# Second-layer experts of a two-layer transformer kernel: weights stand, tokens move, features on partitions

## What is computed

```python
logits = xf @ gate_w + gate_b
scores = softmax(logits)
top_vals, top_idx = top_k(scores, 2)
cw = (one_hot(top_idx, 16) * top_vals[..., None]).sum(axis=1)
h = einsum('td,edh->teh', xf, w1) + b1
g = einsum('td,edh->teh', xf, w3) + b3
a = silu(h) * g
y = einsum('teh,ehd,te->td', a, w2, cw) + cw @ b2
```

## Time and profile before

| | |
|---|---|
| median of 3 runs | 506.08 us (505.69 to 508.32) |
| the profiled execution | 501.9 us, of it the span of the trace 500.2 us |
| TensorE busy, matmuls | 421.4 us (84% of the span), 2573 instructions |
| TensorE busy, weight loads | 316.4 us (63%) |
| VectorE busy | 362.5 us (72%) |
| ScalarE busy | 280.8 us (56%) |
| GpSimd busy | 253.4 us (51%) |
| mean granted TensorE clock | 0.946 of full speed |

### The profile page before, as it was taken

How to read it: one execution, slowest core, us unless ns; L and a number is a source line. 1 busy time by engine, 2 the same in 40 slices (tenths; PEclk the granted TensorE clock), 3 DMA queues, 4 the chain that set the end, 5 groups by cost and what they waited for, 6 DMA issues and landing times.

```text
span 500.2 us, 11175 instructions
## 1 busy us (share of the span) xinstructions
PE 421.4 (84%) x2573; PEld 316.4 (63%) x2573; DVE 362.5 (72%) x1185; ACT 280.8 (56%) x753; POOL 253.4 (51%) x340
## 2 busy tenths in 40 slices
PE   3979762396999999569999999999897969999994
PEld 3567651296999998236556556656554556777774
DVE  5859884052665666489999999999966536777774
ACT  2447540142555554277888888888655245665551
POOL 4014767031545445425545686785666027666562
PEclk9999955597999999799999999999999999999998
DMA  8912425666677686662142161000001321222217
GB/s 230 283 14 56 72 65 116 134 155 166 169 191 209 182 260 203 157 177 72 33 106 68 48 166 55 11 23 11 13 23 43 98 64 46 76 78 80 62 50 227
DMA packets 62321, 53.67 MB, mean 107 GB/s; under 512 B 9677, under 2 KB 51710, under 8 KB 62131
## 3 DMA queue, kind: packets, MB, share of 16 engines
q1 hardware_dynamic: 55330, 42.97, 33.4%
q0 software_dynamic: 5056, 8.48, 5.1%
q10 hardware_dynamic: 1872, 1.52, 1.3%
HBM read 41.15 MB, written 13.73 MB: 110 GB/s over the span
## 4 chain that ended last, share of the span: by engine, by line
PE 28%; DVE 25%; issue 16%; POOL 9%; SPq 9%; DMA 8%; ACT 4%; DVEq 0%; POOLq 0%; ACTq 0%
POOL results L854 6%; PE bank L1847 4%; PE bank L1800 3%; DVE qk_sums L1422 3%; PE bank L1906 3%; PE bank L1815 3%; DVE sums L1445 3%; POOL sorted_tokens L839 3%; PE bank L1946 2%; DVE big L1415 2%; DVE work L1459 2%; SPq L592 2%; SPq L678 2%; DMA results<-work 2%; DMA big<-in_W 2%
## 5 line engine op out<-in xcount | busy, mean ns | idle before, releaser
L854 POOL DMA_INDIRECT results<-work x94 | 92.3, 982 | 96.1 <-DVE work L1379 67.7
L1847 PE MATMUL bank<-late,work 128*128 128x512 f32 x192 | 92.6, 612 | 2.6 <-ACT work L1014 2.4
L990 ACT ACTIVATE work<-bank,mcol 128x128 f32<-128x128 f32 x94 | 43.0, 457 | 72.7 <-PE bank L1792 72.7
L1359 DVE TENSOR_SCALAR work<-bank,b_columns 128x128 f32<-128x128 f32 x94 | 28.7, 347 | 35.9 <-PE bank L1800 35.8
L1847 PEld LDWEIGHTS bank<-late,work 128*128 128x128 f32 x192 | 33.7, 195 | 32.5 <-issue 29.1
L1800 PE MATMUL bank<-work,big 128*128 128x128 f32 x376 | 53.3, 288 | 0.0
L1815 PE MATMUL bank<-big,work 128*128 x376 | 51.0, 280 | 0.1
L1800 PEld LDWEIGHTS bank<-work,big 128*128 128x128 f32 x376 | 49.1, 204 | 0.1
L1815 PEld LDWEIGHTS bank<-big,work 128*128 128x128 f32 x376 | 47.1, 197 | 0.3 <-issue 0.3
L999 ACT ACTIVATE work<-bank,b_columns 128x128 f32<-128x128 f32 x94 | 29.4, 363 | 29.1 <-PE bank L1800 29.1
L1792 PE MATMUL bank<-ident,work 128*128 128x128 f32 x94 | 27.0, 287 | 18.5 <-DMA work<-sorted_tokens 10.2
(11 more groups left out here) (254 smaller groups left out, 1003.5 us busy)
## 6 DMA issues: line engine op xcount, KB each, us to landing
big<-in_W SPq DMA_DIRECT2D x47, 256.0 KB, 2.7
work<-sorted_tokens SPq DMA_DIRECT2D x94, 65.0 KB, 1.9
big<-in_w SPq DMA_DIRECT2D x48, 88.0 KB
big<-results SPq DMA_DIRECT2D x14, 256.0 KB, 3.7
sorted_tokens<-zeros SPq DMA_DIRECT2D x26, 65.0 KB, 2.6
late<-in_WqkvbT SPq DMA_DIRECT2D x1, 1544.0 KB
results<-work POOLq DMA_INDIRECT x94, 2.9
bias_big<-in_b1e SPq DMA_DIRECT2D x16, 88.0 KB
```

Of the source, the lines that this page charges most:

```text
L854: pool.indirect_dma_start(ys[l], bass.IndirectOffsetOnAxis(xg[b][:, D:D + 1].bitcast(I32), 0), yo[b], None, bounds_check=TOPK * T - 1, oob ...
L990: act.activation(xgT[b % 2], bank[:, ends[b % 2], 0:P], ACT.Identity, bias=scale_shift[0], scale=scale_shift[1]).then_inc(e_xTc, 1)
L1847: last = pe.matmul(bank[:, 2 * k + i, :], h3T[b], Wqkvb[:, k * HD + i * 512:k * HD + (i + 1) * 512], start=True, stop=True)
```

## The change

The hidden features of 176 are cut into a part of 112 and a part of 64. The weights of an expert are laid out in four pieces (w1 part A, w3 part A, w3 part C, w1 part C) and stand in TensorE, the tokens move, 128 columns; features come out on partitions. Three products take the place of one: both C parts share the third stationary block (w3's on partitions 0 to 63, w1's on 64 to 127). The activations need no turning back. Biases b1 and b3 are columns: silu takes its bias in ScalarE's instruction, and VectorE adds the other and multiplies in one instruction per part. The output bias b2 is one more row of w2 (row 112) against a row of ones in the activations, which GpSimd writes once. The weights of a slot are copied by VectorE from the looked-up place into a ring of four fixed places, from which TensorE loads them. The order of TensorE's list is now look-up, turn, hidden, output (lag 3). Bias rows come by four more DMAs at the start; the spread biases are no longer loaded (seven DMAs per expert for six).

The diff, cut to its core:

```diff
@@ build
+        HA, HC = 112, H1 - 112
+        parts13 = [(0, 0, HA), (1, 0, HA), (1, HA, HC), (0, HA, HC)]
+        part_at = [0, HA, 2 * HA, 2 * HA + HC]
+        b13r = sb("b13_rows", [E, 2 * H1])
+        NF = 4
+        w13r = sb("w13_ring", [P, NF, 2 * H1])
+        b13c = sb("b13_columns", [P, 3, E])
@@ sync, at the start
+            for (k, a, m), to in zip(parts13, part_at):
+                sp.dma_start(b13r[:, to:to + m], (b1e, b3e)[k][:, a:a + m]).then_inc(ld_w0, 16)
@@ sync, weights1
-                    for k, (w, bias) in enumerate(((w1, b1e), (w3, b3e))):
-                        sp.dma_start(w13v[:, e, k, :], w[e, :, :].rearrange("e d h -> d e h")).then_inc(ld_w1, 16)
-                        sp.dma_start(bv[:, e, k, :], bias[e, :].rearrange("(a e) h -> a e h", a=1)
-                                     .to_broadcast([P, 1, H1])).then_inc(ld_w1, 16)
-                    sp.dma_start(w2s.rearrange("p (e c d) -> p e c d", e=E, c=2)[:, e, :, :],
-                                 w2[e, :, :].rearrange("e (c p) d -> p e c d", p=K1)).then_inc(ld_w1, 16)
-                    sp.dma_start(b2B[:, :].rearrange("p (e d) -> p e d", e=E)[:, e, :],
-                                 b2e[e, :].rearrange("(a e) d -> a e d", a=1).to_broadcast([P, 1, D])).then_inc(ld_w1, 16)
+                    for (k, a, m), to in zip(parts13, part_at):
+                        sp.dma_start(w13v[:, e, to:to + m],
+                                     (w1, w3)[k][e, :, a:a + m].rearrange("e d h -> d e h")).then_inc(ld_w1, 16)
+                    sp.dma_start(w2v[0:HA, e, 0, :], w2[e, 0:HA, :].rearrange("e p d -> p e d")).then_inc(ld_w1, 16)
+                    sp.dma_start(w2v[HA:HA + 1, e, 0, :], b2e[e, :].rearrange("(a e) d -> a e d", a=1)).then_inc(ld_w1, 16)
+                    sp.dma_start(w2v[0:HC, e, 1, :], w2[e, HA:H1, :].rearrange("e p d -> p e d")).then_inc(ld_w1, 16)
@@ gpsimd, between the gates and the diagonals
+            pool.wait_ge(f_one, 2)
+            for b in range(2):
+                pool.memset(hbT[b][P - 32:P, 0:P], 1.0).then_inc(f_one, 1)
+            pool.wait_ge(f_one, 4)
@@ scalar, tokens
-                    after(act, e_h, l * SLOTS + t - 1)
+                    after(act, e_h, l * SLOTS + (1 + l) * (t - 1))
@@ scalar, second layer
-            run_slots(act, SLOTS, NX, [(2, silu), (0, tokens(1, router1["ss"])), (3, act_turned)])
+            def silu_parts(t, b, q, e):
+                act.wait_ge(e_h, SLOTS + 2 * t + 1)
+                after(act, e_act, 2 * (t - 1))
+                act.activation(hb[b % 2][0:HA, 0:P], bank[0:HA, 1 + b % 2, 0:P], ACT.Silu,
+                               bias=b13c[0:HA, 0, bass.ds(e, 1)]).then_inc(e_silu, 1)
+                act.activation(hb[b % 2][0:HC, P:2 * P], bank[P - HC:P, 1 + b % 2, P:2 * P], ACT.Silu,
+                               bias=b13c[P - HC:P, 2, bass.ds(e, 1)]).then_inc(e_silu, 1)
+
+            run_slots(act, SLOTS, NX, [(0, tokens(1, router1["ss"])), (0, None), (1, silu_parts)],
+                      table(mybir.EngineType.Activation, tbl, P, E - 1))
@@ vector, ahead of the first layer's experts
+            dve.tensor_copy(b13c[0:HA, 0:2, :].rearrange("p k e -> p (k e)"), bank[0:HA, 3, E * C0:E * C0 + 2 * E])
+            dve.tensor_copy(b13c[:, 2, :], bank[:, 3, E * C0 + 2 * E:E * C0 + 3 * E])
@@ vector, second layer (result1, biased and gated fall away)
+            def scaled_result1(t, b, q, e):
+                dve.wait_ge(e_o, SLOTS + t + 1)
+                after(dve, e_y[b], moved(1, t))
+                dve.tensor_tensor(yo[b], bank[:, 5 + b % 2, 0:D], gB[:, 1, 1, :], ALU.mult).then_inc(e_yo, 1)
+
+            def gated_parts(t, b, q, e):
+                dve.wait_ge(e_h, SLOTS + 2 * t + 2)
+                dve.wait_ge(e_silu, 2 * t + 1)
+                dve.wait_ge(e_o, SLOTS + t - 1)
+                dve.scalar_tensor_tensor(hbT[b % 2][0:HA, 0:P], bank[0:HA, 3 + b % 2, 0:P], b13c[0:HA, 1, bass.ds(e, 1)],
+                                         hb[b % 2][0:HA, 0:P], ALU.add, ALU.mult).then_inc(e_act, 1)
+                dve.wait_ge(e_silu, 2 * t + 2)
+                dve.scalar_tensor_tensor(hbT[b % 2][0:HC, P:2 * P], bank[0:HC, 1 + b % 2, P:2 * P],
+                                         b13c[0:HC, 2, bass.ds(e, 1)], hb[b % 2][0:HC, P:2 * P],
+                                         ALU.add, ALU.mult).then_inc(e_act, 1)
+
+            def fetch_weights(t, b, q, e):
+                after(dve, e_h, SLOTS + 2 * (t - NF + 1) if t >= NF else 0)
+                dve.tensor_copy(w13r[:, t % NF, :], w13s[:, bass.ds(e * 2 * H1, 2 * H1)]).then_inc(e_hb, 1)
+
+            dve.wait_ge(f_one, 4)
-            run_slots(dve, SLOTS, NX, [(5, result1), (1, biased), (5, scaled_result1), (2, gated), (0, None)], experts)
+            run_slots(dve, SLOTS, NX, [(0, None), (0, fetch_weights), (4, scaled_result1), (2, gated_parts)], experts)
@@ tensor, slot_hidden1
-                after(pe, e_hb, SLOTS + t - 1)
-                pe.matmul(bank[:, 1 + b % 2, 0:2 * H1], xgT[b % 2], w13s[:, bass.ds(e * 2 * H1, 2 * H1)],
+                after(pe, e_act, 2 * (t - 1))
+                pe.wait_ge(e_hb, SLOTS + t + 1)
+                w = w13r[:, t % NF, :]
+                pe.matmul(bank[0:HA, 1 + b % 2, 0:P], w[:, 0:HA], xgT[b % 2],
+                          start=True, stop=True)
+                pe.matmul(bank[:, 1 + b % 2, P:2 * P], w[:, 2 * HA:2 * H1], xgT[b % 2],
+                          start=True, stop=True).then_inc(e_h, 1)
+                pe.matmul(bank[0:HA, 3 + b % 2, 0:P], w[:, HA:2 * HA], xgT[b % 2],
                           start=True, stop=True).then_inc(e_h, 1)
@@ tensor, ahead of the first layer's experts
+            for k, (at, m) in enumerate(((0, HA), (HA, HA), (2 * HA, 2 * HC))):
+                pe.transpose(bank[0:m, 3, E * C0 + k * E:E * C0 + (k + 1) * E], b13r[:, at:at + m], ident[0:E, 0:E])
@@ tensor, second layer (slot_turn_act falls away)
             def slot_out1(t, b, q, e):
-                pe.wait_ge(e_hTc, SLOTS + t + 1)
-                after(pe, e_yb, SLOTS + t - 1)
+                pe.wait_ge(e_act, 2 * (t + 1))
+                after(pe, e_yo, SLOTS + t - 1)
+                pe.matmul(bank[:, 5 + b % 2, 0:D], hbT[b % 2][0:HA + 1, 0:P],
+                          w2s[0:HA + 1, bass.ds(e * 2 * D, D)], start=True, stop=False)
+                pe.matmul(bank[:, 5 + b % 2, 0:D], hbT[b % 2][0:HC, P:2 * P],
+                          w2s[0:HC, bass.ds(e * 2 * D + D, D)], start=False, stop=True).then_inc(e_o, 1)
-            run_slots(pe, SLOTS, NX, [(1, slot_hidden1), (0, None), (0, slot_turn(1)), (3, slot_turn_act),
-                                      (4, slot_out1)], experts)
+            run_slots(pe, SLOTS, NX, [(0, None), (0, slot_turn(1)), (1, slot_hidden1), (3, slot_out1)], experts)
```

More of the change, by code:

```diff
@@ L103, in build @@
     H1 = w1.shape[2]
-    K1 = H1 // 2
     HS = sw1.shape[1]
@@ L248, in build @@
         hbT = [work[:, 3360 + H0 * b:3360 + H0 * (b + 1)] for b in range(2)]
-        act1 = [work[:, 4384 + 176 * b:4384 + 176 * b + H1] for b in range(2)]
         sh_at = ob + 12 * D
@@ L255, in build @@
         last_rows = SC[-1][1]
+        W0_LOADS, W1_LOADS, L1_LOADS = 16 * (2 + 4 + E), 16 * 7 * E, 16 * (4 + 2 * (1 + len(SC)) + len(SC) + 1)
         s_consts = sem("constants_made")
@@ L1118, in _ @@
             act.preload_act_table_set("silu_and_others")
-            def silu(t, b, q, e):
-                act.wait_ge(e_hb, SLOTS + t + 1)
-                after(act, e_hT, t - 1)
-                act.activation(act1[b % 2], hb[b % 2][:, 0:H1], ACT.Silu).then_inc(e_silu, 1)
-            def act_turned(t, b, q, e):
-                act.wait_ge(e_hT, t + 1)
-                act.wait_ge(e_o, SLOTS + t - 1)
-                act.copy(hbT[b % 2][0:K1, 0:2 * P], bank[0:K1, 3 + b % 2, 0:2 * P]).then_inc(e_hTc, 1)
-            run_slots(act, SLOTS, NX, [(2, silu), (0, tokens(1, router1["ss"])), (3, act_turned)])
+            def silu_parts(t, b, q, e):
[7 more added lines that the diff above has]
+                      table(mybir.EngineType.Activation, tbl, P, E - 1))
             for h in range(NT // 2):
@@ L1965, in _ @@
             pe.wait_ge(t_ready, 2)
-            def slot_turn_act(t, b, q, e):
-                pe.wait_ge(e_act, t + 1)
-                after(pe, e_hTc, SLOTS + t - 1)
-                for c in range(2):
-                    last = pe.transpose(bank[0:K1, 3 + b % 2, c * P:(c + 1) * P], act1[b % 2][:, c * K1:(c + 1) * K1],
-                                        ident[:, :])
-                last.then_inc(e_hT, 1)
-            def slot_out1(t, b, q, e):
-                pe.wait_ge(e_hTc, SLOTS + t + 1)
-                after(pe, e_yb, SLOTS + t - 1)
-                for c in range(2):
-                    last = pe.matmul(bank[:, 5 + b % 2, 0:D], hbT[b % 2][0:K1, c * P:(c + 1) * P],
-                                     w2s[:, bass.ds(e * 2 * D + c * D, D)], start=(c == 0), stop=(c == 1))
```

(11 more changed lines are left out.)

32 lines of the change are left out of this document (8 added, 24 removed).

## The result

| | before | changed |
|---|---|---|
| median of the runs | 506.27 us (505.69 to 508.32, 4 runs) | 499.63 us (497.13 to 501.48, 4 runs) |
| ratio | | 0.9884, 95% interval 0.9835 to 0.9933 |
| profiled execution, its span | 501.9, 500.2 us | 499.19, 497.4 us |
| mean granted TensorE clock in it | 0.946 | 0.938 |

The change is faster, by 1.2% (0.7 to 1.7%). The median lies 2.9 us above the forecast of 496.7 us and inside the range of 492.5 to 503. The time alone doesn't tell the forecast (493 to 500 with its bounds) from the rival *producers stay slow* (499 to 503); the profile does, and it is the rival's.

A forecast was written before the change was run, and what follows sets the result against it. A ring of turn, modulation and hidden product bounds the last expert stage; afterwards GpSimd's 1.285 us a slot does. Scatter 39 saves 9.9 us, the tail clock costs 0.5: 9.4 off 501.9 gives 492.5, plus 4.2 offset 496.7 us (492.5 to 503).

The forecast's parts named there:

- producers stay slow: Rival, last expert stage: waits, looked-up addresses and silu keep slots at 1.45 to 1.6 us, 499 to 503 us; chance 0.13.
- TensorE after: Last expert stage: a changed slot is 11 TensorE instructions of 0.11 us, 1.22, taken as 1.25.
- the stall: Before an early scatter, GpSimd idles 2.21 us in place of 0.30; these 1.9 us are no longer made up.
- GpSimd's floor: Scatters of the last expert stage: GpSimd needs 1.285 us a slot and becomes the bound.
- The start: Ahead of the scatters: memsets and a wait add 0.35 us, copies meeting diagonals 0.3 (0 to 2.5).
- The tail clock: After the slots TensorE idles some 6 us, its clock falls, and the last sums start slow: 0.5 us (0 to 2).
- The other engines: Per slot, hidden under 1.285 us: ScalarE 1.08; VectorE 1.34 of durations, about 1.1 with overlap.
- The new ring: Hidden product, output, VectorE's result and gated parts, back to the hidden product: 2.4 us for two slots, 1.2 each.
- The lock: VectorE's fp32 SBUF copies and GpSimd's indirect DMAs block each other by the skill's rule; the forecast counted nothing for it.
- both rivals built on it: Copies hold up scatters: 508 us, chance 0.09; scatters hold up copies: 517 us, chance 0.06.
- The old ring: Kernel before, last expert stage: turn, modulation, hidden product and next turn set the period, 1.61 us a slot.
- The offset: The median of runs, 506.08 us, lies 4.2 us above the profiled execution; kept for the forecast.

The follow-up runs named there:

- late diagonals: VectorE and ScalarE make the diagonals behind their last slots, not GpSimd ahead of its scatters: kernel with 128 rows 489.78 us, kernel before 505.37 us.
- the turn first: The kernel before with one line changed: TensorE turns the tokens ahead of the hidden product; 504.31 us, ratio 0.9977.
- two blocks of 64 rows: The changed kernel with its first output product cut to 64 rows as well, rows 64 to 112 left out of the result; 555.89 us.
- with 128 rows: The changed kernel with its second output product over 128 rows in place of 64, the added activation rows zero; 493.78 us, ratio 0.9793.
- two of 65 rows: The kernel whose second output product takes 65 rows, with its first cut to 65 too, rows 65 to 112 left out; 492.40 us, ratio 0.9678.
- The kernel with the spread biases: The changed kernel also loading the kernel before's spread biases, three loads per expert, into places nothing reads; 500.84 us, ratio 0.9918.

## Why the prediction came out as it did

The number came out inside its range, and not for the reasons given. **The step that failed** is *TensorE after*: "a slot is 1 + 6 + 4 = 11 instructions of 0.11: 1.22 us", taken as 1.25. The price of an instruction was read off blocks of 128 rows and laid on one of 64. The slot took 1.558, and 1.22 as soon as that block had 65 rows or more. That the time still lies within 2.9 us of the forecast is in part luck: two terms of the sum were too dear (the stall and the tail below, 3 us together) and took back some of it. The rival of slow producers priced this case rightly (at 1.55, some 501), but for reasons that don't hold: looked-up addresses, waits and silu cost nothing here (the look-up was moved to no effect; with the 64-row block gone all three are still there at 1.22).

The Trainium skill, page "TensorEngine Tiling (Array Packing)", lists two tiles of 64 rows by 128 columns as a mode of its own (Available Configurations), meant for a contraction over at most 64 rows (When to Use Tiling), and says that changing the tiling mode drains TensorE (Key Properties). The runs agree in each point that they can test: the cost is there at 64 rows and gone at 65, 96 and 128, the weight load loses its cover on entering and on leaving, and two blocks in a row pay once. That an ordinary product over 64 rows switches the mode is my inference: the page doesn't say so, and no row names the mode. The page has no price either; here it is 0.34 us a round trip at full clock, 0.49 at half. The prediction weighed rules on SBUF and had passed over this one, which spoke against the change.

**GpSimd's floor** of 1.285 was right: 1.28 to 1.29 wherever results were ahead. With 65 rows or more the stage went as the sum had it, and better: 80.0 us from the gates to the end for a forecast of 91.5 - 9.4 = 82.1. The difference is in three terms.

**The stall** of 1.9 us "comes out of hiding" didn't. Behind the second scatter the changed kernel spends 1.42 in place of 1.28. The gap was read as GpSimd's own, counted from the scatter before; it counts from the third result, which in the kernel before was made on time, by VectorE's row:

```profile
420.60 0.28 DVE L1585 TENSOR_TENSOR work<-work,gB 128x128 f32<-128x128 f32 x1
```

It ends at 420.88, and the scatter starts at 423.26, 2.38 us behind it, where from slot 8 to 42 a scatter starts 0.77 to 0.78 behind its result. So VectorE, which the row names as releaser, had long been done. The same 2.38 or 2.39 stands in both kernels with late diagonals, with the turn first and with two blocks of 64 rows. In the changed kernel the third result was there 3.99 us ahead of its scatter, behind the diagonals, and covers it. With the diagonals gone it is ahead by less, and 1.3 us of the gap shows. What those 1.6 us are (the prediction points at an instruction fetch) wasn't tested.

**The start**: scatter 0 was to come 0.65 later, and came 1.2 later behind the gates (11.06 for 9.86). Memsets and wait cost 0.40 for 0.35, the diagonals 0.79 (10.20 for 9.41) for 0.3, inside the bound of 2.5. **The tail clock** fell as forecast where TensorE ended early (with 128 rows, half clock from 479.6 to 486.4), but cost nothing that shows: from scatter 39 to the end it was 17.9 to 18.1 us in all kernels with 65 rows or more, whether 3.4 us of half clock fell there (late diagonals) or 10.2 (65 rows), and 19.1 before, where the sum had 19.6. In the kernels at full clock whose producers are the bound it is 19.1 to 19.3, but 18.5 with the turn first. They still have seven slots to finish behind slot 39, and VectorE and TensorE sum only behind those; that would fit the 1 us, and wasn't tested.

**The other engines** were right: copies of 0.354 for 0.35, results 0.291 for 0.29, gated parts 0.350 and 0.334 for 0.35, in the rows of 430 to 460 us:

```profile
L1597 DVE COPY w_ring<-big 128x352 f32 x19 | 6.7, 354 | 0.9
L1588 DVE SCALAR_TENSOR_TENSOR work<-bank,b_columns,work 112x128 f32<-112x128 f32 x19 | 6.7, 350 | 0.0
L1591 DVE SCALAR_TENSOR_TENSOR work<-bank,b_columns,work 64x128 f32<-64x128 f32 x19 | 6.3, 334 | 0.1
L1582 DVE TENSOR_TENSOR work<-bank,gB 128x128 f32<-128x128 f32 x20 | 5.8, 291 | 6.5 <-PE bank L1991 6.5
```

VectorE and ScalarE keep up with 1.22 a slot. The terms of *The new ring* add up to 2.48 and not 2.4, 1.24 a slot; since passes took 1.22 the ring held no more than that. **The lock** between copies and scatters didn't appear: scatters of 0.98, copies of 0.34 to 0.53 in the changed kernel (0.32 to 0.62 with 128 rows, the median 0.344 and 0.345), and 43 copies taken away change a scatter by 0.01. For fp32 copies of 352 columns beside indirect DMAs of 128 rows, the rule of the Trainium skill, page "SBUF — State Buffer" (the trap where VectorE blocks DMA), doesn't hold on these traces; the measurement decides, and both rivals built on it were rightly rated low.

**The old ring** was rightly read, but it wasn't alone: with it opened, the next one closed at 1.57. The sum didn't suffer, as the change removes both. **The offset** of 4.2 us between the profiled execution and the median was rightly kept: the profile of before had a mean clock of 0.946, and the line of 0.41 us for 0.001 puts it some 2.5 us below an execution at 0.940. The rest of the 4.2 stays open.

**The accounts**, from the gates on: forecast 9.4 saved; the stall gives 1.5 back (50.5 us from scatter 0 to 39 with 128 rows, for 52.0), the tail 1.5, the start takes 0.6: 11.8. The kernel with the 64-row block is slower than that by 5.7 to 6.7 between scatters 0 and 39 (56.3 and 57.2 for 50.5) and by 1.2 in the tail. That leaves 4 to 5.

## What to carry to other kernels

Price a TensorE instruction by rows of its own row count: one product over 64 rows between products over more costs 0.34 us each time here, so pad it with one row of zeros. Two such products next to each other paid once, but in the one execution that had them TensorE stayed at half clock, so that isn't a way to recommend. When a stage has a producer and a consumer, set each start of the consumer beside the end of the result that it takes, rather than trust the releaser that the row names; a pile of finished results covers a delay that counts from the result. Compare stages from a common event and runs at equal granted clock before a few us are blamed on an edit.

## What was not expected of the hardware

**Row counts and the clock.** With two blocks of 64 rows among the six of a slot, the granted clock stayed at half (1.2 GHz) from 410.4 us to about 547 us of the span, although TensorE shows no idle time between 412 and 542 us; with two of 65 rows it was at full (2.4 GHz), and with one of 64 it was at full, or back at full within about 8 us of the gates, in all four profiles that had it. The first is one execution against four of the second (mean clock 0.827 against 0.923 to 0.940), and it wasn't repeated. The kernel with the spread biases, with one such block, once ran at a mean clock of 0.645 (627.45 us), beside nine executions at 0.931 to 0.951. So a low clock for long comes without the second block too, and whether the row counts or the single execution held it down stays open.

**The clock elsewhere.** Half-clock stretches at the joints of the attention part come and go between executions of one kernel (of the two profiles of the changed kernel one has such a stretch near 362 us, the other not). Time and mean clock go together, and over the 61 executions of the kernel before they move by 13 us, more than this change gives.
